# Ten gather slots instead of five in the edge passes of a graph network, index tiles staged two iterations ahead, and SP's loads and stores in five pieces

## What is computed

```python
x = _layernorm(x + _L0_gnn_ref(...))   # segment_max over dst of relu([x_i, x_j - x_i] @ W1 + b1) @ W2 + b2
x = _layernorm(x + _L1_gnn_ref(...))   # mean of edge_attr over src, concatenated to x, two dense layers
x = _layernorm(x + _L2_gnn_ref(...))   # segment_sum of x[src] over dst, mean, gate, @ W_lin.T + b_lin
x = _layernorm(x + _L3_gnn_ref(...))   # attention: typed k, v of src, q of dst, softmax over dst, typed output
```

## Time and profile before

| | us |
|---|---|
| median of 3 runs (lowest to highest) | 21960.21 (21959.04 to 21966.19) |
| the profiled execution: its span | 21982.3 |
| pass a and what is before it | 0 to 6170 |
| to_starts | 6170 to 6288.5 |
| pass b, first to last gather | 6288.5 to 11055.3 |
| nodes of layers 0 and 1 | 11055.3 to 11484.3 |
| pass c | 11484.3 to 15844.6 |
| nodes of layer 2, tables of layer 3 | 15844.6 to 16782.2 |
| pass d | 16782.2 to 21556.0 |
| nodes of layer 3 | 21556.0 to 21982.3 |

### The profile page before, as it was taken

The page is one execution under the profiler, slowest core; times in us unless marked ns, Lnnn a source line. Parts: engine busy times, 40 slices in busy tenths (PEclk is TensorE's granted clock), DMA queues, the critical chain, the costliest instruction groups (busy, mean ns, idle before and its releaser), DMA issues. The chain is left out here.

```text
span 21982.3 us, 148548 instructions
## 1 busy us (share of the span) xinstructions
PE 4774.0 (22%) x30182; PEld 4149.9 (19%) x30182; DVE 6911.8 (31%) x16401; ACT 1772.2 (8%) x6281; POOL 15097.0 (69%) x13304
## 2 busy tenths in 40 slices
PE   4444444444423333333320000000041000000002
PEld 4444444444412222222210000000031000000001
DVE  3333333333312222222241111111122444444444
ACT  1111111111100000000010000000021000000001
POOL 5888888888876666666657777777724666666664
PEclk8555555555555555555555555555576555555555
DMA  4444444444422222222231111111122222222222
GB/s 93 53 52 52 52 52 53 50 53 52 52 48 65 65 65 65 63 65 64 65 59 48 47 47 46 47 47 46 43 68 89 87 89 89 87 90 87 89 89 38
DMA packets 1456154, 1380.95 MB, mean 63 GB/s; under 512 B 777810, under 2 KB 1260924, under 8 KB 1455996
## 3 DMA queue, kind: packets, MB, share of 16 engines
q0 software_dynamic: 775408, 541.25, 17.1%
q1 hardware_dynamic: 662716, 736.98, 10.3%
q10 hardware_dynamic: 18000, 102.41, 1.1%
HBM read 762.18 MB, written 617.56 MB: 63 GB/s over the span
## 5 line engine op out<-in xcount | busy, mean ns | idle before, releaser
L500 POOL DMA_INDIRECT agg<-sums,ag_idx x3125 | 4984.9, 1595 | 1166.4 <-issue 1118.5
L534 POOL DMA_INDIRECT gat<-tab_t,gi x3125 | 3021.6, 967 | 1752.5 <-issue 928.0
L534 POOL DMA_INDIRECT gat<-tab_b,gi x3125 | 3014.6, 965 | 1752.6 <-issue 931.3
L534 POOL DMA_INDIRECT gat<-tab_x,gi x3125 | 3299.2, 1056 | 1100.9 <-issue 1061.1
L842 PE MATMUL bank<-at,same 128*128 128x64 f32 x6250 | 1882.7, 431 | 3281.7 <-issue 1057.3
L842 PEld LDWEIGHTS bank<-at,same 128*128 128x128 f32 x6250 | 1570.5, 311 | 3419.7 <-issue 1813.5
L908 PE MATMUL pair<-ident,tails 128*64 128x128 f32 (+1 forms) x20 | 4.9, 419 | 9304.2 <-DVE tails L1209 4931.4
L908 PEld LDWEIGHTS pair<-ident,tails 128*64 128x64 f32 (+1 forms) x20 | 3.0, 167 | 9305.2 <-DVE tails L1209 4931.6
L1302 DVE TENSOR_TENSOR run_sb<-p,gat 128x320 f32<-128x320 f32 x625 | 317.1, 507 | 3710.6 <-DMA gat<-tab_x,gi 3710.6
L1164 DVE TENSOR_TENSOR run_sb<-p,bank 128x320 f32<-128x320 f32 x625 | 304.9, 488 | 3177.7 <-remote 2346.6
L876 PE MATMUL bank<-ident,ub 128*128 128x128 f32 x1250 | 413.0, 434 | 3494.1 <-DVE ub L1192 2228.1
(11 more groups left out here) (263 smaller groups left out, 13806.5 us busy)
## 6 DMA issues: line engine op xcount, KB each, us to landing
edge<-start_rows SPq DMA_DIRECT2D x250, 800.0 KB
run<-run_sb SPq DMA_DIRECT2D x250, 800.0 KB
run<-run_sb SPq DMA_DIRECT2D x125, 900.0 KB
start_rows<-zeros ACTq DMA_DIRECT2D x125, 800.0 KB, 3.5
at<-in_edge_attr SPq DMA_DIRECT2D x125, 800.0 KB
tab_t<-trow SPq DMA_DIRECT2D x98, 512.0 KB, 2.6
agg<-sums,ag_idx POOLq DMA_INDIRECT x3125
gat<-tab_b,gi POOLq DMA_INDIRECT x3125
```

The lines of the kernel that those rows point to most:

```text
L500: pool.indirect_dma_start(agg_d[r], rows(agg_d[r], ag_idx[:, k, r:r + 1]), sums[:, k, r, :], None, bounds_check=AGR - 1, oob_is_err=True, ...
L534: pool.indirect_dma_start(gat[:, k, s, 0:width], None, table, rows(table, gi[tp][:, s, k:k + 1])).then_inc(g_in[c][k], 16)
```

## The change

- `gat` holds ten slots in b and c (its row of 2 x 64 is used in halves); in d the second five lie in `side`, which is free then. Each slot has its semaphore (`g_in[tp][k]`), shared by the three passes. Gather (t, k) waits for the use of (t-2, k); t = 0 and t = 1 are written out without that wait.
- `gi[tp]` for t+2 is written by ACT at the end of iteration t (in c after DVE's last step of t); `ct` and `pn` stay where they were. One semaphore `gi_st` counts the index tiles of all passes. `src_i` and `t_idx` are 5 columns wider.
- Each load and store of SP is made as five DMAs, one for each s. The first two of an iteration go out as before, the others wait for one, two and three more steps.
- Pass d also waits for the scatters of `to_starts`, since they read `side`.

```diff
-        g_in = {c: [sem(f"{c}_gat{i}") for i in range(KS)] for c in "bcd"}
+        g_in = [[sem(f"gat_in{i}{k}") for k in range(KS)] for i in range(2)]
+        gi_st = sem("gi_staged")
...
         def sides(t, tp):
-            return t * 8 + (16 if tp == 0 else 8)
+            return t * (8 * SUB) + (16 * SUB if tp == 0 else 8 * SUB)
+
+        def room(t, tp):
+            return t * (8 * SUB) + (8 * SUB if tp == 0 else 0)
...
+        def gslot(c, tp, k):
+            if c == "d":
+                half = gat[:] if tp == 0 else side[:, 0:2 * KS * SUB, :].rearrange(
+                    "p (k s a) f -> p k s (a f)", k=KS, s=SUB)
+                return half[:, k]
+            return gat[:].rearrange("p k s (a f) -> p (k s a) f", a=2)[:, (tp * KS + k) * SUB:(tp * KS + k + 1) * SUB, :]
+
+        PACE = [max(s - 1, 0) for s in range(SUB)]
...
-                def load(t, tp):
-                    sp.dma_start(edge0[tp][:].rearrange("p s k f -> p s (k f)"),
-                                 chains(starts_d)[:, :, bass.ds(t * (KS * F), KS * F)]).then_inc(e_in[c][tp], 16)
...
+                def load(t, tp, s):
+                    sp.dma_start(edge0[tp][:, s].rearrange("p k f -> p (k f)"),
+                                 chains(starts_d)[:, s, bass.ds(t * (KS * F), KS * F)]).then_inc(e_in[c][tp], 16)
...
                 def body(t, tp):
-                    if with_side:
-                        sp.wait_ge(side_done, t * KS)
-                        load(t + 1, 1 - tp)
-                    sp.wait_ge(run_done, t * KS)
-                    store(t - 1, 1 - tp)
+                    for s in range(SUB):
+                        if with_side:
+                            sp.wait_ge(side_done, t * KS + PACE[s])
+                            load(t + 1, 1 - tp, s)
+                        sp.wait_ge(run_done, t * KS + PACE[s])
+                        store(t - 1, 1 - tp, s)
...
-            def gathers(c, table, width, staged, per, used):
+            def gathers(c, table, used):
                 def body(t, tp, first):
-                    pool.wait_ge(staged, (t + 1) * per)
+                    pool.wait_ge(gi_st, t + (EDGES[c] * (T + 2) + 1))
...
-                            pool.wait_ge(used, t * KS + (k - KS + 1))
+                            pool.wait_ge(used, t * KS + (k - 2 * KS + 1))
...
-                            pool.indirect_dma_start(gat[:, k, s, 0:width], None, table,
-                                                    rows(table, gi[tp][:, s, k:k + 1])).then_inc(g_in[c][k], 16)
-                each_iteration(pool, body)
+                            pool.indirect_dma_start(out_rows[:, s, :], None, table,
+                                                    rows(table, gi[tp][:, s, k:k + 1])).then_inc(g_in[tp][k], 16)
+
+                body(0, 0, True)
+                body(1, 1, True)
+                with loop(pool, 2, T - 1, 2) as t:
+                    body(t, 0, False)
+                    body(t + 1, 1, False)
+                body(T - 1, 0, False)
...
             def phase_b(t, tp, first):
...
-                        stage("b", b_st, src_i, t + 1, 1 - tp, True)
+                        stage(b_st, t + 1, 1 - tp, True)
+                stage_index(src_i, t + 2, tp)
...
             def phase_c(t, tp, first):
                 if not first:
                     act.wait_ge(c_s, t * KS)
-                stage("c", c_st, src_i, t + 1, 1 - tp, False)
+                stage(c_st, t + 1, 1 - tp, False)
+                act.wait_ge(c_s, t * KS + KS)
+                stage_index(src_i, t + 2, tp)
```

More of the change, by code:

```diff
@@ L296, in sides, with turns, landed @@
         def sides(t, tp):
-            return t * 8 + (16 if tp == 0 else 8)
+            return t * (8 * SUB) + (16 * SUB if tp == 0 else 8 * SUB)
+        def room(t, tp):
+            return t * (8 * SUB) + (8 * SUB if tp == 0 else 0)
+        def turns(tp):
+            return (T + 1 - tp) // 2
+        EDGES = {"b": 0, "c": 1, "d": 2}
+        def landed(c, t, tp):
+            return t * (8 * SUB) + ((16 if tp == 0 else 8) * SUB + EDGES[c] * turns(tp) * 16 * SUB)
+        def gslot(c, tp, k):
[5 more added lines that the diff above has]
+        PACE = [max(s - 1, 0) for s in range(SUB)]
         def loop(eng, *bounds):
@@ L388, in edge_io, with store @@
             def edge_io(c, side_done, run_done, run_d, width, with_side):
[L390 to L403 removed]
+                def load(t, tp, s):
+                    sp.dma_start(edge0[tp][:, s].rearrange("p k f -> p (k f)"),
+                                 chains(starts_d)[:, s, bass.ds(t * (KS * F), KS * F)]).then_inc(e_in[c][tp], 16)
+                def store(t, tp, s):
+                    sp.dma_start(chains(run_d)[:, s, bass.ds(t * (KS * width), KS * width)],
+                                 run_view(tp, width)[:, s].rearrange("p k f -> p (k f)")).then_inc(r_out[c][tp], 16)
+                def body(t, tp):
+                    for s in range(SUB):
[4 more added lines that the diff above has]
+                        store(t - 1, 1 - tp, s)
                 if with_side:
[L406 to L407 removed]
+                    for s in range(SUB):
+                        load(0, 0, s)
+                    for s in range(SUB):
+                        load(1, 1, s)
                 with loop(sp, 1, T - 3, 2) as t:
@@ L412, in edge_io @@
                 sp.wait_ge(run_done, (T - 1) * KS)
-                store(T - 2, 1)
+                for s in range(SUB):
+                    store(T - 2, 1, s)
                 sp.wait_ge(run_done, T * KS)
-                store(T - 1, 0)
+                for s in range(SUB):
+                    store(T - 1, 0, s)
                 for tp in range(2):
-                    sp.wait_ge(r_out[c][tp], 16 + 16 * ((T + 1 - tp) // 2))
+                    sp.wait_ge(r_out[c][tp], 8 * SUB + 16 * SUB * turns(tp))
             def carry_out(n, car, width):
@@ L557, in node_rows @@
                         batch(b + i, i)
-            gathers("b", tab_b, F, b_st, 3, b_u)
+            gathers("b", tab_b, b_u)
             node_rows("1", run0, car0, F, 0)
             pool.wait_ge(n_out["1"], 16 * NBAT)
-            gathers("c", tab_x2, F, c_st, 2, c_s)
+            gathers("c", tab_x2, c_s)
             node_rows("2", run2, car2, F, 1)
@@ L566, in _ @@
                 pool.wait_ge(t_o[i], 16 + 8 * NT)
-            gathers("d", tab_t, 2 * F, d_st, 3, d_wm)
+            pool.wait_ge(scat, 2 * 16 * NT)
+            gathers("d", tab_t, d_wm)
             node_rows("3", run3, car3, ROW3, 2)
@@ L629, in _, with stage_index, stage @@
             each_iteration(act, phase_a)
-            def stage(c, st, index, t, tp, with_pen):
+            def stage_index(index, t, tp):
+                act.activation(gi[tp][:], index[:, :, bass.ds(t * KS, KS)], ACT.Copy).then_inc(gi_st, 1)
+            def stage(st, t, tp, with_pen):
                 cs = bass.ds(t * KS, KS)
-                act.activation(gi[tp][:], index[:, :, cs], ACT.Copy).then_inc(st, 1)
                 act.activation(ct[tp][:], cont[:, :, cs], ACT.Copy).then_inc(st, 1)
@@ L831, in reduce_cols @@
                 if k == 0:
-                    pe.wait_ge(a_ld[tp], sides(t, tp))
+                    pe.wait_ge(a_ld[tp], t * 8 + (16 if tp == 0 else 8))
                 pe.wait_ge(a_su, n + 1)
@@ L1007, in _ @@
             v.memset(nt_i[:], 0).then_inc(zeroed, 1)
-            for sems in (r_out["b"], r_out["c"], r_out["d"], t_o, l_out):
+            for sems in (r_out["b"], r_out["c"], r_out["d"]):
+                for q in sems:
+                    token().then_inc(q, 8 * SUB)
+            for sems in (t_o, l_out):
                 for q in sems:
```

50 lines of the change are left out of this document (29 added, 21 removed).

## The result

22494.17 us median (22463.61 to 22502.47, 4 runs) against 21960.13 us for the kernel before in the same visit to the chip: ratio 1.0238 [1.0224, 1.0253], 534 us slower. The prediction (21290 us, 3.1% faster) was wrong in its sign.

The account below looks back on a forecast made before the run. It took POOL's waits in b and d, for a DVE with slow signals, as the bound. 21982.3 - 712 + 38 = 21308 us for the profiled execution, 22 us over the runs' median, gave 21290 us, range 20,200 to 22,700.

Parts of the forecast that it names:

- What bounds the kernel: In b and d POOL waits for other engines, 438.8 + 380.9 us and 819.0 us; in c it never does.
- Part 3: In b and d: POOL's rest falls to 8.2 us, two iterations take 70.7 us for 76.4; together 712 us saved.
- q/2.35: POOL's rest in two iterations of d, q being its quick issuing time: 13.2 us of rest bought about 31 us.
- Slow when POOL has issued for about 30 us: Signals become slow when POOL has issued without a rest for about 30 us, and a rest clears them.
- b gets the same: Pass b, with d's period and nearly its steps (3.5 us quick, 17.5 slow), saves 356 us as d does.
- The second way: b and d at the length of c, where POOL never rests, would give 407 + 413 = 820 us.
- Part 5: SP's loads and stores in five pieces: taken as zero, at most 1344 us in b and in d, 672 in c.
- The slower rival: SP's 128 more posts an iteration slow the signals: 25,300 us at 84 ns a post, 22,130 at a quarter; chance 0.28.
- Nothing gained: Short rests clear nothing; POOL only lies further ahead, then waits as long: 21,960 us, chance 0.12.
- The prediction's own signs of being wrong: Pass c moving by more than 100 us, or DVE's steps being quick throughout.
- Part 4: End of each pass: DVE may have five more steps after the last gather, 19 us a pass, 38 us back.
- POOL's own pace: DVE rides over slow signals with more slots; b and d take 31.25 us an iteration: 20,230 us, chance 0.20.

Follow-up runs that it names:

- e7: Changed kernel (ten slots, earlier index tiles) but SP's loads and stores whole, at the slow level: 22378.84 us, ratio 1.0183 to the kernel before.
- e8: Kernel before with only SP's loads and stores in five pieces, at the slow level: 22028.79 us, ratio 1.0025.
- e2: Kernel before with only SP's loads and stores in five pieces, at the quick level: 19875.9 us, ratio 1.0007.
- e9: Kernel before with POOL held to two steps ahead of DVE, at the slow level: 21493.57 us, ratio 0.9783.
- e3: Kernel before with POOL held to two steps ahead of DVE, at the quick level: 20109.51 us, ratio 1.0127.
- e1: Changed kernel with SP's loads and stores whole, at the quick level: 19861.7 us, ratio 1.000 to the kernel before.
- e10: Kernel before, slow level: b drained before each iteration, c gathers 16 words a row for 64, d without loads after the first two; 22197.07 us.

## Why the prediction was wrong

- **What bounds the kernel** was read rightly for the slow level: POOL's rests for a DVE with slow signals in b and d. That the slow signals come and go with the visit was not to be seen in one trace, and it voids every term at the other: there the kernel before already takes 19861 us.
- **Part 3 is the step that failed**: the balance for two iterations of d, which counted the whole of POOL's rest as quick time and let it cost q/2.35. Its split of POOL's 63 us was nearly right, 19.2 us quick and 43.3 slow against 17 and 46.8 in the rows above. The rest was wrong, 8.2 us against 16.1. The rows show that signals stay slow into the rest, for 6.9 us after POOL's stop at 19111.9 (and about as long in the kernel before, 4.9 us after its stop at 19136.8, 6.5 in the median). The balance had 27.4 us for 7.2 quick steps and 43.3 us for 2.8 slow steps; the rows have six quick steps in 24.2 us and four slow steps in 54.9, the last of them over POOL's stop. Before, three slow steps took 41.2 us and the seven others 35.0. In POOL's 63 us DVE does 7 to 8 steps in both kernels, so the added stock brings nothing there. It only lets DVE take its steps at 3.8 us, and then those of 15 us begin sooner, 17 us after POOL's restart instead of 26.8.
- **"Slow when POOL has issued for about 30 us"** does not hold as a rule: in the changed kernel it is 17 us, after a rest of 16.1 us, no shorter than those before. The number of quick steps between slow steps moves less, mostly seven in d before and six after. Whether the start is set by what DVE has done or posted, the runs do not settle.
- **"b gets the same"** failed worst. The prediction took 17.5 us as b's slow step; the full one is 23.1 us in both kernels. Of two short rests in two iterations the change makes one long one, and steps over 20 us went from 33 to 109. e7 gives 295 us to b against 42 to d.
- **The second way** (c's pace for b and d) rested on POOL alone; c has two DVE instructions a step, and none of its steps is over 9 us in either kernel, so its length says nothing of a pass that waits for DVE.
- **Part 5, zero for SP's pieces**, was off by 56 us alone and by 108 to 128 beside the slots (514 to 534 less 406). The slower rival, alone in having the sign right, named the pieces, which make the smaller part: 17 ns a post was its point of decision, 680 us over the three passes, and 56 us are 1.4 ns. c, which it named as the witness, did not slow down (4345.80). The Trainium skill, "DMA: Bandwidth & Descriptors", Rules for kernel authors, says to coalesce many small transfers into one large one. e8 goes that way: 2500 more DMAs cost 56 us, 22 ns each, and at the quick level e2's 12 us are within its interval. The 5000 us that the prediction made of that page's fixed cost of about 2 us (section Anatomy of one DMA) were an estimate for DMAs of POOL's kind that nothing covers; here SP issues them, and nearly all of it is covered.
- **Nothing gained** was the nearest rival. Its reason, that POOL only lies further ahead and then waits as long, is what the rows show, with a wait even longer: 1127 us in b and 954 in d, where the prediction looked for about 500. The prediction's own signs of being wrong did not show, as c moved by 14.5 us and slow steps remained, so they could not tell a gain from a loss.
- **Part 4**, the tails, was 55 us for 38. The rival of **POOL's own pace** is what the quick level shows, 3914 to 3977 us a pass, but there it holds for the kernel before as well.

## What to carry to other kernels

Where signals between engines are slow while one of them issues, as in these traces, more buffers need not bring producer and consumer nearer: here the consumer spent its quick time sooner and the producer rested longer. Try the lead in both directions, since it is one constant in a wait. At the slow level less was worth 2.2% (e9), and at the quick level the same edit cost 1.3% (e3), so measure at both. Before a sum is made from waits in one trace, ask whether those waits are the kernel's or the visit's: the same kernel took 19861 and 21972 us.

## What the runs showed of the hardware

The same kernel differs by 10.6% between visits to the chip, steadily within each. The granted clock is not the difference: it is 0.50, the lower level of 1.2 GHz, in the windows of b at both. At the slow level a wait of DVE on its own result takes 1.23 us, as here between L1453 and L1457 of the changed kernel; in its pass d 216 of 625 such waits are over 1 us, and 101 in the kernel before. In e1's pass d, at the quick level, none is over 0.13 us. POOL's gathers in c run with 1.40 us from one to the next at the slow level, and 1.25 us at the quick one. Both levels were met under the same chip number, so it need not be a property of one chip; what sets it is not known.

```profile
19117.41 0.19 DVE L1453 TENSOR_TENSOR run_sb<-mp,ar 128x20 f32<-128x20 f32 x1 [2.90 <-remote]
19118.83 0.19 DVE L1457 TENSOR_TENSOR dm<-mp,run_sb 128x20 f32<-128x20 f32 x1 [1.23 <-DVE run_sb L1453]
```

The slow pace of the gathers in c does not depend on their bytes (e10). Nor do their transfers start later: counted in the DMA packets of c, the last packet of a gather starts 1.18 us, in the median, after POOL has issued it, in the changed kernel at the slow level and in e1 at the quick one.
